# Last attention of a four-block chain: four energy banks, and a max pass in single banks

## The reference, cut to what matters

```python
qkv = (h @ Wqkv.T + bqkv).reshape(B, N, 16, 16, 3)
energy = jnp.einsum('bhqd,bhkd->bhqk', q, k)          # 1024 x 1024 for each of 2 x 16 heads
att = jax.nn.softmax(energy, axis=-1) / D ** 0.5
out = jnp.einsum('bhqk,bhkd->bhqd', att, v)
out = out.reshape(B, N, D) @ Wp.T + bp
h1 = out + hidden
return _sln(h1, ...) + h1
```

## Time and profile before

| what | value |
|---|---|
| median of three runs | 1013.05 us |
| the profiled execution's own time | 1012.53 us |
| its span, first to last instruction | 1010.7 us |
| PE busy | 901.2 us (89%) |
| DVE busy | 663.8 us (66%) |
| ACT busy | 433.8 us (43%) |
| mean granted clock of TensorE | 0.94 |

### The profile page before, as it was taken

The page is one execution under the profiler, slowest core; times in us unless marked ns, Lnnn a source line. Parts: engine busy times, 40 slices in busy tenths (PEclk is TensorE's granted clock), DMA queues, the critical chain, the costliest instruction groups (busy, mean ns, idle before and its releaser), DMA issues.

```text
span 1010.7 us, 12522 instructions
## 1 busy us (share of the span) xinstructions
PE 901.2 (89%) x4692; PEld 515.0 (51%) x4692; DVE 663.8 (66%) x1101; ACT 433.8 (43%) x768; POOL 227.2 (22%) x332
## 2 busy tenths in 40 slices
PE   3698899999989798789989678999999999999992
PEld 0356688875445444578875334433333333333431
DVE  6796766772110521485373478799999989999476
ACT  1020323233223123333323121788787878788660
POOL 2824200230000300040022031023223332223432
PEclk9698999999989899899999778799999999999996
DMA  9343200020000000000005962014415154201011
GB/s 336 124 147 106 86 1 1 1 84 5 1 0 1 0 1 1 0 1 1 1 1 122 173 134 98 1 30 69 73 28 80 37 74 67 36 19 29 23 42 42
DMA packets 27068, 52.37 MB, mean 52 GB/s; under 512 B 7738, under 2 KB 15404, under 8 KB 26750
## 3 DMA queue, kind: packets, MB, share of 16 engines
q1 hardware_dynamic: 20928, 41.52, 17.6%
q0 software_dynamic: 6080, 10.05, 3.5%
HBM read 38.48 MB, written 10.72 MB: 49 GB/s over the span
## 4 chain that ended last, share of the span: by engine, by line
PE 71%; DVE 12%; DMA 7%; ACT 3%; issue 3%; POOL 2%; SPq 1%; DVEq 0%; ACTq 0%; POOLq 0%
PE PA L1246 10%; PE PA L1257 10%; PE PD L1086 8%; PE PA L1064 7%; PE PA L1139 6%; PE PA L1000 6%; PE PD L1112 5%; PE PD L1009 5%; PE PD L1228 4%; DMA row_sums<-TG 3%; DVE NMX L1705 2%; DVE ST L1427 2%; PE PA L992 2%; DVE XN L1438 2%; PE PD L1000 1%
## 5 line engine op out<-in xcount | busy, mean ns | idle before, releaser
L1705 DVE TENSOR_REDUCE NMX<-PD 128x2 f32<-128x1024 f32 x256 | 301.4, 1219 | 34.6 <-PE PD L1228 30.1
L896 ACT ACTIVATE R<-PA 128x512 f32<-128x512 f32 x512 | 266.9, 603 | 72.9 <-PE PA L1246 71.7
L1246 PE MATMUL PA<-STKR 50*128 50x512 f32 x512 | 185.2, 454 | 4.5 <-ACT R L896 3.4
L1228 PE MATMUL PD<-STKR 48*128 48x512 f32 x512 | 150.6, 460 | 15.4 <-DVE NMX L1705 8.3
L1246 PEld LDWEIGHTS PA<-STKR 50*128 50x128 f32 x512 | 83.0, 188 | 151.4 <-ACT R L896 138.1
L1086 PE MATMUL PD<-WHR,HSR 128*128 128x256 f32 x512 | 98.9, 292 | 7.6 <-DVE HSR L1617 4.9
L826 ACT ACTIVATE R<-PA,VEC 128x512 f32<-128x512 f32 x64 | 43.7, 687 | 131.3 <-PE PA L1064 108.3
L1064 PE MATMUL PA<-XSR,WHR 128*128 128x512 f32 x256 | 83.8, 410 | 11.3 <-issue 5.3
L1086 PEld LDWEIGHTS PD<-WHR,HSR 128*128 128x128 f32 x512 | 84.7, 197 | 14.2 <-DVE HSR L1617 5.5
L1228 PEld LDWEIGHTS PD<-STKR 48*128 48x128 f32 x512 | 62.1, 190 | 41.4 <-DVE NMX L1705 19.1
L1086 PE MATMUL PD<-WLR,HSR 128*128 128x256 f32 x256 | 73.9, 289 | 0.0
(11 more groups left out here) (244 smaller groups left out, 1160.2 us busy)
## 6 DMA issues: line engine op xcount, KB each, us to landing
STKR<-qk_parts SPq DMA_DIRECT2D x96, 128.0 KB, 6.8
R<-in_l_w SPq DMA_DIRECT2D x8, 1024.0 KB, 5.5
W<-in_w SPq DMA_DIRECT2D x4, 1024.0 KB, 10.1
qk_parts<-PARTS SPq DMA_DIRECT2D x8, 512.0 KB, 7.9
qk_parts<-PARTS POOLq DMA_DIRECT2D x8, 512.0 KB, 3.2
R<-in_wcond SPq DMA_DIRECT2D x1, 3584.0 KB, 11.4
S<-row_reciprocals POOLq DMA_DIRECT2D x56, 64.0 KB, 2.1
X<-in_x SPq DMA_DIRECT2D x4, 512.0 KB, 13.1
```

What stands on the lines that cost most here:

```text
L896: act.activation(PB[:, n % 2, j, :], PA[:, e % NEB, :], ACT.Exp).then_inc(s_exp3, 1)
L1228: i = pe.matmul(PD[:, o + h, :], QS[rows, gg % NSLOT, jj, q0:q0 + P], KS[rows, gg % NSLOT, jj, kc * HALF:(kc + 1) * HALF], start=True, sto ...
L1246: pe.matmul(PA[:, e % NEB, :], KS[rows, gg % NSLOT, jj, kt * P:(kt + 1) * P], QS[rows, gg % NSLOT, jj, c * HALF:(c + 1) * HALF], start=Tru ...
L1705: ve.tensor_reduce(out, PD[:, o:o + NROW, :], axis=AX_X, op=ALU.max, negate=True).then_inc(s_mred, 1)
```

## The change

Energy products go round in four banks, PA 0 to 2 and PD 3. The max pass goes round in the three banks that are left, PD 0 to 2, one matmul to a bank: a max job becomes two, one for each row group, each with its own semaphore increment, its own reduction over 512 columns on DVE (128 x 512 to 128 x 1), and its own slot. So there are 512 reductions in place of 256, over the same columns. In the text M0 to M3 are the four max matmuls of a step. A job waits for the reduction of the job three before it.

The order in a step on TensorE becomes: the V product of the step before, a turn if there is one, E3, M0, M1, E0 and E1 of the next step, M2, M3, E2 of the next step. An energy product waits for the exp of the product four before it.

The jobs `p3`, `hd` and `hx` of the last steps (from number `LATEJ` on) go round in three banks too. The earlier jobs of PD keep four.

```diff
-NEB = 3
+NEB = 4
+NMB = 3
...
     if stage == "mx":
-        return [("max", n)]
+        return [("max", n, h) for h in range(NROW)]
...
+    LATEJ = min(n for (_, tag, *_), n in DJ.items() if tag in ("hd", "hx", "p3"))
+
+    def dslot(n):
+
+        return n % 4 if n < LATEJ else (n - LATEJ) % NMB
...
+        EB = [PA[:, 0, :], PA[:, 1, :], PA[:, 2, :], PD[:, NMB, :]]
...
-                    act.activation(PB[:, n % 2, j, :], PA[:, e % NEB, :], ACT.Exp).then_inc(s_exp3, 1)
+                    act.activation(PB[:, n % 2, j, :], EB[e % NEB], ACT.Exp).then_inc(s_exp3, 1)
...
-            def pair_bank(*job):
+            def max_bank(*job):
 
                 n = MJ[job]
-                if n >= 2:
-                    pe.wait_ge(s_mred, n - 1)
-                return n % 2 * 2
+                if n >= NMB:
+                    pe.wait_ge(s_mred, n - NMB + 1)
+                return n % NMB
...
+                rows = slice(h * HROW, h * HROW + KSTK)
+                pe.matmul(PD[:, o, :], QS[rows, gg % NSLOT, jj, q0:q0 + P],
+                          KS[rows, gg % NSLOT, jj, kc * HALF:(kc + 1) * HALF], start=True, stop=True).then_inc(s_mfull, 1)
+
+            def max_lead(n):
                 for h in range(NROW):
-                    rows = slice(h * HROW, h * HROW + KSTK)
-                    i = pe.matmul(PD[:, o + h, :], QS[rows, gg % NSLOT, jj, q0:q0 + P],
-                                  KS[rows, gg % NSLOT, jj, kc * HALF:(kc + 1) * HALF], start=True, stop=True)
-                i.then_inc(s_mfull, 1)
+                    maxpass(n, h)
...
                     energy(0, 0)
                     energy(0, 1)
-                energy(n, 2)
+                    energy(0, 2)
                 if n >= 1:
                     times_v(n - 1)
                 if n in TURN:
                     turn_max(TURN[n])
                 energy(n, 3)
-                more = [x for tag, x in max_jobs("step", n) if tag == "max"]
-                for x in more[:1]:
-                    maxpass(x)
+                more = [x for tag, *x in max_jobs("step", n) if tag == "max"]
+                for x in more[:2]:
+                    maxpass(*x)
...
-                for x in more[1:]:
-                    maxpass(x)
+                for x in more[2:]:
+                    maxpass(*x)
+                if n + 1 < NSTEP:
+                    energy(n + 1, 2)
...
-                out = NMX[:, m % 2, kc, jj * NROW * TPC + t:(jj + 1) * NROW * TPC:TPC]
-                ve.tensor_reduce(out, PD[:, o:o + NROW, :], axis=AX_X, op=ALU.max, negate=True).then_inc(s_mred, 1)
...
+                o = max_bank("max", n, h)
+                col = (jj * NROW + h) * TPC + t
+                ve.tensor_reduce(NMX[:, m % 2, kc, col:col + 1], PD[:, o, :], axis=AX_X, op=ALU.max, negate=True
+                                 ).then_inc(s_mred, 1)
```

More of the change, by code:

```diff
@@ L203, in max_jobs @@
     if stage == "mx":
-        return [("max", n)]
+        return [("max", n, h) for h in range(NROW)]
     if stage == "step":
         turn = [("turn", TURN[n])] if n in TURN else []
-        return turn + [("max", LEAD + 2 * n + i) for i in range(2) if LEAD + 2 * n + i < NMAX]
+        return turn + [("max", LEAD + 2 * n + i, h) for i in range(2) if LEAD + 2 * n + i < NMAX for h in range(NROW)]
     return [("turn", n)] if stage == "tm" else []
@@ L967, in bank @@
                     hold[kind] = None
-                if n >= 4:
-                    if kind == "a":
+                if kind == "a":
+                    if n >= 4:
                         evacuated(pe, *AORDER[n - 4])
-                    else:
-                        pe.wait_ge(ev, n - 3)
-                return ps[0:rows_, n % 4, :]
+                    return ps[0:rows_, n % 4, :]
+                back = 4 if n < LATEJ else NMB
+                if n >= 4 and not LATEJ <= n < LATEJ + NMB:
+                    pe.wait_ge(ev, n - back + 1)
+                return ps[0:rows_, dslot(n), :]
             def abank(*job, rows_=P):
@@ L1205, in v3, with maxpass @@
                 m.then_inc(s_afull, 1)
-            def pair_bank(*job):
+            def max_bank(*job):
                 n = MJ[job]
-                if n >= 2:
-                    pe.wait_ge(s_mred, n - 1)
-                return n % 2 * 2
-            def maxpass(n):
+                if n >= NMB:
+                    pe.wait_ge(s_mred, n - NMB + 1)
+                return n % NMB
+            def maxpass(n, h):
                 m, r = divmod(n, UNIT)
@@ L1219, in maxpass @@
                 t, kc = divmod(r, NC)
-                if n == 0:
+                if n == 0 and h == 0:
                     pe.wait_ge(s_dev, sd[0])
-                o = pair_bank("max", n)
-                if n % (NC * UNIT) == 0:
+                o = max_bank("max", n, h)
+                if n % (NC * UNIT) == 0 and h == 0:
                     pe.wait_ge(s_stack[gg], STACKED)
                 q0 = c * HALF + t * P
+                rows = slice(h * HROW, h * HROW + KSTK)
+                pe.matmul(PD[:, o, :], QS[rows, gg % NSLOT, jj, q0:q0 + P],
+                          KS[rows, gg % NSLOT, jj, kc * HALF:(kc + 1) * HALF], start=True, stop=True).then_inc(s_mfull, 1)
+            def max_lead(n):
                 for h in range(NROW):
-                    rows = slice(h * HROW, h * HROW + KSTK)
-                    i = pe.matmul(PD[:, o + h, :], QS[rows, gg % NSLOT, jj, q0:q0 + P],
-                                  KS[rows, gg % NSLOT, jj, kc * HALF:(kc + 1) * HALF], start=True, stop=True)
-                i.then_inc(s_mfull, 1)
+                    maxpass(n, h)
             def turn_max(m):
                 pe.wait_ge(s_nmc, m + 1)
-                o = pair_bank("turn", m)
+                o = max_bank("turn", m)
                 pe.transpose(PD[0:UNIT, o, 0:P], NMC[:, :], ident[:, :]).then_inc(s_mfull, 1)
@@ L1245, in energy @@
                 rows = slice(h * HROW, h * HROW + KFULL)
-                pe.matmul(PA[:, e % NEB, :], KS[rows, gg % NSLOT, jj, kt * P:(kt + 1) * P],
+                pe.matmul(EB[e % NEB], KS[rows, gg % NSLOT, jj, kt * P:(kt + 1) * P],
                           QS[rows, gg % NSLOT, jj, c * HALF:(c + 1) * HALF], start=True, stop=True).then_inc(s_efull, 1)
@@ L1323, in _ @@
                  "a2": down("a2", lambda b: GT[:, b], 1, gelu_ready), "f2": f2,
-                 "n3": turn("n3", lambda b: XN[:, b], "f2"), "qk3": qk3, "v3": v3, "mx": maxpass, "tm": turn_max,
+                 "n3": turn("n3", lambda b: XN[:, b], "f2"), "qk3": qk3, "v3": v3, "mx": max_lead, "tm": turn_max,
                  "step": step, "hd": heads_turned, "hx": heads_back, "p3": p3})
@@ L1505, in bank @@
                 ve.wait_ge(s_dfull, n + 1)
-                return PD[0:rows_, n % 4, :]
+                return PD[0:rows_, dslot(n), :]
             def two(j):
@@ L1691, in v3, with max_bank, reduce_max @@
                 i.then_inc(s_aevd, 1)
-            def pair_bank(*job):
+            def max_bank(*job):
                 n = MJ[job]
                 ve.wait_ge(s_mfull, n + 1)
-                return n % 2 * 2
-            def reduce_max(n):
+                return n % NMB
+            def reduce_max(n, h):
                 m, r = divmod(n, UNIT)
@@ L1702, in reduce_max, with lead_max @@
                 t, kc = divmod(r, NC)
-                o = pair_bank("max", n)
-                out = NMX[:, m % 2, kc, jj * NROW * TPC + t:(jj + 1) * NROW * TPC:TPC]
-                ve.tensor_reduce(out, PD[:, o:o + NROW, :], axis=AX_X, op=ALU.max, negate=True).then_inc(s_mred, 1)
-                if n % UNIT == UNIT - 1:
-                    ve.wait_ge(s_mred, MJ[("max", n)] + 1)
+                o = max_bank("max", n, h)
+                col = (jj * NROW + h) * TPC + t
+                ve.tensor_reduce(NMX[:, m % 2, kc, col:col + 1], PD[:, o, :], axis=AX_X, op=ALU.max, negate=True
+                                 ).then_inc(s_mred, 1)
+                if n % UNIT == UNIT - 1 and h == NROW - 1:
+                    ve.wait_ge(s_mred, MJ[("max", n, h)] + 1)
                     ve.tensor_tensor(NMC[:, :], NMX[:, m % 2, 0, :], NMX[:, m % 2, 1, :], ALU.min).then_inc(s_nmc, 1)
+            def lead_max(n):
+                for h in range(NROW):
+                    reduce_max(n, h)
             def turned_max(m):
-                o = PD[0:UNIT, pair_bank("turn", m), 0:P]
+                o = PD[0:UNIT, max_bank("turn", m), 0:P]
                 if m >= 1:
@@ L1725, in step @@
                 m, kt = divmod(n, NT)
-                for tag, x in max_jobs("step", n):
-                    (turned_max if tag == "turn" else reduce_max)(x)
+                for tag, *x in max_jobs("step", n):
+                    (turned_max if tag == "turn" else reduce_max)(*x)
                 if kt == 5 and 1 <= m < NUNIT - 1:
@@ L1768, in _ @@
                  "u1": split("u1"), "d0": d0, "h0": h0, "lb": lb, "qkv": qkv, "att": att, "pr": pr, "d1": d1,
```

(2 more changed lines are left out.)

## The result

The changed kernel takes 1022.1 us (median of four runs, 1018.13 to 1022.7), the kernel before 1012.63 beside it. The ratio is 1.0088, its 95% interval 1.0062 to 1.0114: slower by 0.9%, where +0.4% was forecast. The profiled execution has a span of 1019.7 us, 9.0 more than before.

The account below looks back on a forecast made before the run. The prediction took the loop exp, E2, V, E3 (2.60 us a step) as the bound. Its terms, +7.7 + 2.4 - 0.7 + 0.7 - 0.5 - 5.2, gave +4.4 us: 1017.4 against the median, range 1010 to 1023.

Parts of the forecast that it names:

- E2: Third energy product of a step; with four banks it goes out ahead of V's wait, and the loop loses its slot, 0.43.
- The bound before: Last attention: the loop exp, E2, V, E3 sets a 2.60 us step; without E2's slot it is 2.17.
- The new wait: Steps with max pass: M3 waits for M0's reduction, ahead of E2, V and the next M0; step 2.00 + R, 2.69 us.
- R: DVE's reduction of 512 columns in the new loop, taken as 0.69 us; break-even at 0.65.
- Rival 4: Reduction costs per column only: R = 0.61, step 2.61, -5.4 us, 1007.7; chance 0.07.
- The handover of M0: M0 and its handover to DVE take 0.53 us together; a second handover beside E3's, 0 to 0.03 a step, taken as 0.
- rival 1: M0's handover waits behind E3's, another 0.03 in the loop: 4.4 + 3.4 us, 1020.8; chance 0.12.
- Does DVE keep up: Four single reductions start 0.61 us apart, 2.44 a step, below the step of 2.69, so DVE is not the bound.
- Ahead of the steps: Up to the first V product: max passes +0.7 us and the opening -0.5, together +0.2.
- the opening: Step 0: E3 no longer waits for a bank, an estimated -0.5 us from E2's slot of 0.43.
- Last intervals: After step 114, without max passes: 12 intervals lose E2's slot of 0.43, -5.2 us; steps with an output projection 3.58.
- Waits for the row sums: DVE's reciprocal waits for a DMA three times; it comes 5 x 0.09 later after the copy that starts it: -0.7 us.

Follow-up runs that it names:

- three_jobs: The changed kernel with M3 left out of the steps, a neutral value filled in for its results; 996.13 us, ratio 0.9840 to the kernel before.
- m0_first: The changed kernel with M0 issued just ahead of E3 instead of just behind it; 1021.3 us, ratio 1.0097 to the kernel before.
- fourth_116: The kernel before, with the fourth energy bank and the changed order only from E2 of step 116 on; 1007.95 us, ratio 0.9958.
- lead_four: The changed kernel with max jobs in four single banks ahead of step 0, three only from step 0 on; 1022.86 us, ratio 1.0104 to the kernel before.
- single_four: The kernel before with single max jobs in four slots, three energy banks and the old order; 1012.38 us, ratio 0.9991.
- fourth_late: The kernel before, with the fourth energy bank and the changed order only from E2 of step 115 on; 1013.13 us, ratio 1.0012.
- m1_half: The changed kernel with M1's reduction reading 256 of its 512 columns in every step; 1023.44 us, ratio 1.0113 to the kernel before.
- m3_after_v: The changed kernel with M3 issued behind the V product of the next step instead of ahead of E2; 1063.77 us, ratio 1.0507 to the kernel before.

## Why the prediction was right, and where it was not

The forecast was 1017.4 us in a range of 1010 to 1023; the 1022.1 measured lies in it, 0.9 from its end. The sign and the mechanism came as worked out, the size is about half of what was measured (+4.4 for +9.0 in the span).

- **The bound before** (exp, E2, V, E3): right. three_jobs and the last steps show what is left when E2 goes out of it, 2.18 against the 2.17 worked out.
- **The new wait**: right in every link. M3 waits for M0's reduction of its own step; halving that one moves the step by 0.26, halving its neighbour by nothing.
- **R**: 0.69 was taken, 0.682 measured. Rival 4 (half of the pair's 1.22) is out.
- **The handover of M0**: the term that was mis-sized. The prediction took M0 and handover at 0.53 together, "as E3 is to ACT", and the second handover at 0; the two are 0.565. The step rose by 0.13 (2.61 to 2.74) and not by 0.09. These 0.04, in each of the 114 intervals but those where DVE's own work comes first, are the 4.1 us by which V 0 to V 114 fell short (+9.4 for +13.5), and 0.03 to 0.035 of the 0.04 is the second handover, by m0_first; the rest lies in the other links (0.75 for 0.74) and in rounding. The whole fell short by 4.6: the errors of the other three parts (+1.5, +0.7 and -1.7) nearly cancel, and that is luck. This was rival 1, given 0.12, with 0.03. The Trainium skill, page "TensorE: Matmul & The Clock Gate", section "The cost: per-tile semaphore tail", gives 26.3 ns for each further increment. The trace agrees: 0.03 between the two starts (807.66 and 807.69, and 808.28 and 808.31 the other way round), and m0_first shows that it goes with the second of the two. The argument made against it, M1's handover of 0.04, did not bear on it: there E0 was issued second.
- **Does DVE keep up**: right. Neighbours start 0.60 apart in the lead, and DVE stands 0.26 a step.
- **Ahead of the steps**: wrong. +0.2 was put, +1.7 measured. The nine last pairs cost 0.6 (10.84 for 10.26, 0.7 forecast), the first energy product comes another 0.3 later, and the opening gave 0.4 back (4.49 for 4.85). But that the third slot stops PE in the lead, in front of work that DVE needs, was not looked at; it cost 2.5 us, and 1.3 us of it are hidden by a start that was earlier in this execution.
- **Last intervals**: -4.5 for -5.2. The first projection of each group comes 0.23 late (3.82 for 3.58) and one step is 2.42: E2 is now issued while ACT is close to its full load, and waits for an exp after all.
- **After the last V product**: -1.7, not forecast, and no merit of the change that any run shows. The sixteen matmuls of the last projections took 3.71 us and before 5.39, the clock's upper and lower level. fourth_116, which has the same order there, took 5.24, lead_four 5.39, m0_first 3.71.
- **Waits for the row sums**: -0.7 forecast, -0.7 measured. The direction is borne out, the exact size is luck: the extra time is 1.1 to 2.0 us in the traces of the kernel before, single_four and fourth_late, and 0.1 to 0.7 in those of the changed kernel, m0_first, m1_half and lead_four.

The chances leaned to slower at 0.48 against 0.41 for no change, with the forecast itself just inside no change; the measured +0.9% is on the side that held the more.

## What to carry to other kernels

With n slots and more than n jobs between two passages of a long operation on the same in-order engine, the last job waits for the first one's consumer, and that wait stands in front of the long operation: count jobs per passage before giving a slot away, and write out the loop, link by link. Here four jobs in three slots took 2.74 a step, three in three 2.18, and four in four 2.61, where the old loop through the exp binds. Where two matmuls end together, the one whose consumer is in the loop goes first. A resource that is short only in one phase can change hands at the end of that phase; put the change one step after the last use, not at it (one case, 5 us apart).

## What the runs showed of the hardware

- Two matmuls over 512 columns in different row groups that start within 0.01 us of each other are handed over 0.534 and 0.565 us after their start in the changed kernel, 0.535 and 0.566 in m0_first, in the order of issue (means).
- A reduction of one bank over 512 columns takes 0.682 us, of two banks 1.22; neighbours start 0.60 and 1.13 apart, so four singles cost 2.48 where two pairs cost 2.36.
- PE's granted clock was at 1.2 GHz after a pause of 2.07 us ahead of E2 (fourth_late), 0.7 us after PE was busy again, and came back 10.2 us later. In m3_after_v it was at 1.2 GHz at the start of the stage for nine intervals of 4.59 us and more (41.8 us, PE busy in all of them), in the kernel before for two (4.07 and 4.04); what brought it back is not shown. A load that stood 0.77 us in every plain step (the changed kernel) left it at 2.4 GHz.
